# A decoder layer on one core: where a turn of the attention loop spreads and transposes the cross reciprocals, and when it turns the cross keys

## The chip, the cores and the metric

The kernel runs on one core of a Trainium2 chip. The metric is the device time of one execution in microseconds; the time before is the median of three runs. The engines are TensorE (PE, with its weight loads shown apart as PEld), VectorE (DVE), ScalarE (ACT), GpSimd (POOL) and SyncE (SP), which issues the DMAs. Each has its own instruction stream and they meet through semaphores.

## What is computed

A decoder layer with pre-normalisation on 32 sequences of 128 tokens and 512 features, in float32: causal self-attention (16 heads of 32), cross-attention to a context of 128 tokens with 256 features (32 heads of 16), and a gated feed-forward part with quantised weights.

```python
x = x + self_attention(layernorm(x), Wq, Wk, Wv, Wo)       # rope on q and k, causal
x = x + cross_attention(layernorm(x), ctx, pos, Wq, Wkv, Wout, bout)
#   q = (x @ Wq).reshape(b, n, 32, 16);  k, v = split(ctx @ Wkv)
#   q, k = axial_rope(q, pos), axial_rope(k, pos)
#   w = softmax(q . k / sqrt(16));  out = (w @ v) @ Wout + bout
x = x + ffn(layernorm(x))
```

## The kernel before

`build_decoder` has two phases. `attention_phase` takes one sequence at a time; `ffn_phase` then runs over eight blocks of four sequences. The change touches the first alone.

**Turns.** The attention is a software pipeline. A turn, `turn(sq, cq, nx, nz, oq)`, works on four sequences at once: self-attention of `sq`, cross-attention of `cq` (the sequence before it), the projections of the next one, `nx`, and the end of the cross-attention of `oq`, the one before `cq`. `schedule` writes out four turns, loops over 27 (`fori(2, B - 3)`), writes out one more and closes with `last()`. Each engine has a `turn` of its own with its instructions in a fixed order, so the order in the source is the order on the queue. In the loop the values waited for are in registers.

**Scores and probabilities.** A turn computes three sets of scores into the PSUM banks S[0..3]: "1" (self), "2a" and "2b" (the two halves of the cross heads). For each set DVE takes the row maxima (`row_maxima`, L1180), ACT the 16 exponentials with their row sums (`exponentials`, L949), PE transposes the probabilities (`halves_of_probs`, L553), and DVE (banks 0 and 2, L1186) and ACT (banks 1 and 3, L1014) copy them back to SBUF as probT, which the next product and, in the same banks, the next scores wait for (`collect`).

**Transposes in halves.** A 128x128 transpose can be done as 64-row halves. `halves_of_two` does so for two tiles at once, alternating the upper rows of the one with the lower rows of the other into their two banks; the remaining halves may follow only when the first have been written, for which PE waits on its own semaphore `halves_d`. `transpose_keys_and_probs` puts a group of probabilities between the first halves of the two keys and their second ones.

**Reciprocals.** The row sums of both cross halves are inverted by DVE (`row_sums2`, L1200), spread over the 16 columns of each head by POOL (`spread`, L405, tile rbc2), transposed by PE into the bank TC, copied by ACT to rT2 (`copy_reciprocals`, L955), and multiplied into the attention's output by DVE (`context2`). The same chain with rbc1 and rT1 serves self-attention.

**The end of a turn on PE.** `project_v1` (L666) does the value projection in 12 matmuls, 10 of them (`V1_SPLIT`) ahead of `transpose_keys_and_probs` (L578 for the keys, L553 for the probabilities) and 2 behind. Then come the four full transposes of z2, the normalised input of cross-attention (L497), into TC, and the next turn starts with the masks (L521) and matmuls (L526) of the scores "1". Behind these and the product `attend2("2b")` (L648) stand the four transposes of rbc2 (L497), the q2 projection of z2, and the o2 projection (both L512).

**The end of a turn on the others.** DVE: statistics of x1 (the last is L1103), the maxima of "2b", the ropes of k2 and k1 (L1130 and L1133), the normalisation (L1109 to L1114), a copy of the transposed k2 (L1382), the even copies of "2b", the reciprocal. POOL: the sums of both ropes (L399), the masked copies of k2 for even and odd heads (`key_pairs`, L421), the spread of the reciprocals.

Of the kernel before, what the change touches and what calls it, by code (L numbers as in the profile page):

```python
# [138 lines left out]
def attention_phase(nc, fp32, fp32r, ALU, ACT, AX, x, ctx_in, pos, consts,  # L139
                    wq1, wk1, wv1, wo1, wq2, wkv2, wo2, bout, x2_dram, shared_f, shared, ident, mhalf_c, ffn):  # L140
    es = ExitStack()
    with es:
# [229 lines left out]
        def _(pool):  # L372
# [24 lines left out]
            def rope_sum(n, q):  # L397
                wait(pool, ab[n], q + 1)
                pool.tensor_tensor(RA[n][:, :], RA[n][:, :], RB[n][:, :], ALU.add).then_inc(rot[n], 1)  # L399
# [51 lines left out]
            def turn(sq, cq, nx, nz, oq):  # L451
                if is_first(nx):
                    rope_sum("q1", nx)
                    rope_sum("k1", nx)
                if is_first(sq):
                    split_ctx(sq)
                    rope_sum("q1", nx)
                    spread(1, sq, rinv1, rbc1, H1, DK1)
                    rope_sum("k2", sq)
                if oq is not None:  # L460
                    ctx_low(2, oq)
                if cq is not None:
                    rope_sum("q2", cq)
                if nz is not None:
                    rough_rstd(1, nz)
                if sq is not None and cq is not None:
                    spread(1, sq, rinv1, rbc1, H1, DK1)
                    split_ctx(sq)
                if cq is not None:
                    add_bias(cq)  # L470

                if sq is not None:
                    ctx_low(1, sq)
                if nx is not None and cq is not None:
                    rope_sum("q1", nx)
                if sq is not None:
                    rough_rstd(2, sq)
                    if cq is not None:
                        rope_sum("k2", sq)

                if nx is not None and sq is not None:
                    rope_sum("k1", nx)
                if sq is not None:
                    key_pairs(sq)
                if cq is not None:
                    spread(2, cq, rinv2, rbc2, H2, DK2)

# [6 lines left out]
        def _(pe):  # L494
            def transpose4(dst, src, k=KT):
                for j in range(k):
                    last = nc.tensor.transpose(dst[:, j * P:(j + 1) * P], src(j), ident[:, :])  # L497
                return last
# [161 lines left out]
            V1_STEPS = [(a, w, j) for a, w in ((z1T_h, WHI["v1"]), (z1T_h, WLO["v1"]), (z1T_l, WHI["v1"])) for j in range(KT)]  # L660
            V1_SPLIT = 10

# [38 lines left out]
            def turn(sq, cq, nx, nz, oq):  # L701
# [21 lines left out]
                if has_o:  # L723
                    attend2("2b")
                    pe.wait_ge(rb_r[2], oq + 1)
                    if has_c:
                        pe.wait_ge(zT_hi[2], cq + 1)
                        pe.wait_ge(zT_lo[2], cq + 1)
                    transpose4(TC, columns(rbc2[:, :, :].rearrange("p h d -> p (h d)"))).then_inc(ri_d[2], 1)
                if has_c:  # L730
# [11 lines left out]
                if has_c and not is_first(cq):  # L742
                    if has_o:
                        pe.wait_ge(riT_r[2], oq + 1)
                    project(TC, cxT_h, cxT_l, "kv2", CKT, slice(D, 2 * D)).then_inc(pj["v2"], 1)
# [52 lines left out]
                if has_s:  # L798
                    pe.wait_ge(z_r[2], sq + 1)
                    pe.wait_ge(k2T_c, sq + 1)  # L800
                    transpose4(TC, columns(z2)).then_inc(zT_d[2], 1)
                if in_loop:
# [24 lines left out]
            def last():  # L827
# [6 lines left out]
                pe.wait_ge(zT_lo[2], M + 1)  # L834
                transpose_reciprocals(2, N)
                project_q2(M)
                project_o2(N)
                transpose_q2(M)
                transpose_prob("1", L)
                pe.wait_ge(riT_r[2], N + 1)  # L840
                project(TC, cxT_h, cxT_l, "kv2", CKT, slice(D, 2 * D)).then_inc(pj["v2"], 1)
# [70 lines left out]

            LOOP_HALVES = 8
            before = {"n": 0}
# [13 lines left out]
        def _(act):  # L928
# [11 lines left out]

            def exponentials(u, q, banks=range(G)):
                rs = (rsum1, rsum2)[kind(u) - 1]
                if u != "2b" and 0 in banks:
                    wait(act, ri_r[kind(u)], q)
                for c in banks:
                    act.wait_ge(nmax_r[kind(u)], G * nth(u, q) + c + 1)
                    for i in range(G):
                        h = head(u, c, i)
                        last = nc.scalar.activation(prob[:, c, i, :], S[c][:, i * P:(i + 1) * P], ACT.Exp,  # L949
                                                    bias=nmax[:, c, i:i + 1], accum_out=rs[:, h:h + 1])  # L950
                    last.then_inc(p_r[kind(u)], 1)

            def copy_reciprocals(n, q):
                act.wait_ge(ri_d[n], q + 1)
                nc.scalar.activation((rT1, rT2)[n - 1][:, :], TC[:, :], ACT.Copy).then_inc(riT_r[n], 1)  # L955

# [10 lines left out]
            def last():  # L967
                exponentials("1", L, (0,))
                copy_reciprocals(2, N)
                exponentials("1", L, (1, 2, 3))  # L970
                copy_q2(M)
# [48 lines left out]
            def turn(sq, cq, nx, nz, oq):  # L1020
                has_s, has_c, has_n, has_o = sq is not None, cq is not None, nx is not None, oq is not None
                if has_s:
                    exponentials("1", sq, (0,))
                if has_o:
                    copy_reciprocals(2, oq)
                if has_s:
                    exponentials("1", sq, (1, 2, 3))
                if has_c:
# [4 lines left out]
                if has_c:  # L1033
                    copy_v2(cq, TC)
                    exponentials("2a", cq, (0,))
                if has_s:
                    copy_reciprocals(1, sq)
# [4 lines left out]
                if has_c:  # L1042
                    exponentials("2a", cq, (1, 2, 3))
                    odd_copies("2a", cq)
# [18 lines left out]
                if has_s:  # L1063
                    act.wait_ge(zT_d[2], sq + 1)
                    nc.scalar.activation(flat(z2T_h), TC[:, :], ACT.Copy).then_inc(zT_hi[2], 1)
                if is_first(nx):
                    z1T_high(nz)
# [17 lines left out]
        def _(dve):  # L1085
# [223 lines left out]
            def turn(sq, cq, nx, nz, oq):  # L1309
# [58 lines left out]
                if has_s:  # L1368
                    dve.wait_ge(x1_r, sq + 1)
                    statistics(2, x1A, sq)  # L1370

                if has_c:
                    row_maxima("2b", cq, range(G))
                if has_s and has_c:
                    rope("k2", sq, TC, DK2, *axial(sq), 1.0)
                if has_n and has_s and has_c:
                    rope("k1", nx, PA, DK1, cos1, sin1, 1.0)
                if has_s:
                    normalise(2, x1A, z2, sq)
                if has_s:  # L1380
                    dve.wait_ge(rT_d["k2"], sq + 1)
                    nc.vector.tensor_copy(RA["k2"][:, :], TC[:, :]).then_inc(k2T_c, 1)  # L1382
                if has_c:
                    even_copies("2b", cq)
                if has_c:
                    row_sums2(cq)
                if has_s:
# [408 lines left out]
```

## Time and profile before

| what | us |
|---|---|
| median of 3 runs (1676.98 to 1678.65) | 1677.18 |
| the profiled execution's own time | 1680.36 |
| its span, first to last instruction | 1678.5 |
| PE busy | 1625.0 (97%) |
| DVE busy | 1162.9 (69%) |
| ACT busy | 967.3 (58%) |
| POOL busy | 548.4 (33%) |

The time of the profiled execution is its span and 1.9 us around it; it lies 3.2 us above the median. The busy time of PE is modelled from the size of its matmuls, which are pipelined, so a busy PE need not be at its peak. In a row of the timeline the first number is the start in us from the span's start, the second the time from the start of the first to the end of the last instruction of the row, and in brackets stands idle time ahead of it with what ended it.

### The profile page before, as it was taken

To read this page: it belongs to the slowest core of one execution; us is meant where nothing else is said; L and a number is where in the kernel's file an instruction comes from. 1 tells how busy PE (TensorE), PEld (TensorE's weight loads), DVE (VectorE), ACT (ScalarE), POOL (GpSimd) and SP (SyncE) were. 2 spreads that over 40 slices of the span, in tenths; PEclk is the share of its full clock that TensorE was granted. 3 is DMA by queue.
4 is the path that set the end of the run, shared out by engine and by line. 5 is a ranking of instruction groups with operands and counts; after the bars stand their busy time and mean duration, and the time that the engine had idled before them with its cause. 6 is when DMAs were issued, how large, how long until landed. Compare 5 with 4: busy or idle time off the path is not lost. (4 is left out here: it accounts for less than half of the span.)

```text
span 1678.5 us, 42062 instructions
## 1 busy us (share of the span) xinstructions
PE 1625.0 (97%) x15216; PEld 1267.4 (76%) x15216; DVE 1162.9 (69%) x2087; ACT 967.3 (58%) x3847; POOL 548.4 (33%) x535
## 2 busy tenths in 40 slices
PE   6899999999999999999999999998999999999997
PEld 4677777777777777777777777766888888888885
DVE  7788788888888888888888878786744344344332
ACT  5577677777777777777767777675422222222221
POOL 4344443444444444444444444341011011011011
PEclk9999999999999999999999999998999999999999
DMA  6011111111110011111111011022420120120110
GB/s 215 29 32 31 36 34 50 30 30 36 41 43 30 30 36 47 37 30 36 30 54 30 30 36 33 23 70 90 150 76 26 50 75 25 50 75 25 50 50 26
DMA packets 55098, 81.00 MB, mean 48 GB/s; under 512 B 4880, under 2 KB 25488, under 8 KB 55056
## 3 DMA queue, kind: packets, MB, share of 16 engines
q1 hardware_dynamic: 55056, 80.43, 14.7%
q8 instruction: 28, 0.46, 0.1%
q14 instruction: 14, 0.11, 0.0%
HBM read 63.63 MB, written 16.78 MB: 48 GB/s over the span
## 5 line engine op out<-in xcount | busy, mean ns | idle before, releaser
L949 ACT ACTIVATE prob<-bank,nmax 128x128 f32<-128x128 f32 x1536 | 539.9, 408 | 155.8 <-DVE nmax L1180 151.7
L949 ACT ACTIVATION_READ_ACCUMULATOR prob<-bank,nmax 128x1 f32 x1536 | 380.7, 248 | 0.0
L1588 PE MATMUL fbank<-shared,piece_hi 128*128 128x512 f32 x1152 | 280.3, 394 | 0.0
L1180 DVE TENSOR_REDUCE nmax<-bank 128x4 f32<-128x512 f32 x376 | 233.5, 683 | 64.8 <-PE bank L536 51.2
L1588 PEld LDWEIGHTS fbank<-shared,piece_hi 128*128 128x128 f32 x1152 | 215.8, 187 | 53.2
L399 POOL TENSOR_TENSOR rope_buf<-rope_buf 128x512 f32<-128x512 f32 x128 | 165.6, 1303 | 159.7 <-DVE rope_buf L1133 159.6
L1740 DVE SCALAR_TENSOR_TENSOR h<-fbank,su_c,sil 128x512 f32<-128x512 f32 x88 | 66.0, 750 | 200.1 <-PE fbank L1588 197.1
L1674 ACT ACTIVATE sil<-fbank,sg_c 128x512 f32<-128x512 f32 x88 | 60.5, 687 | 174.8 <-PE fbank L1588 172.2
L1680 ACT ACTIVATE h_h<-h 128x512 fp32r<-128x512 f32 x88 | 55.6, 632 | 175.1 <-DVE h L1740 175.1
L449 POOL TENSOR_TENSOR cn_l<-cn,cn_h 128x512 fp32r<-128x512 f32 x64 | 82.8, 1294 | 211.9 <-DVE cn L1172 211.9
L512 PE MATMUL bank<-shared,z1T_h 128*128 128x512 f32 x520 | 140.4, 412 | 4.5 <-ACT shared L932 2.6
L1186 DVE COPY probT<-bank 128x512 f32<-128x512 f32 x186 | 119.3, 683 | 23.4 <-PE bank L553 23.3
L1571 POOL TENSOR_TENSOR xr<-xr,ys 128x512 f32<-128x512 f32 x32 | 40.2, 1288 | 288.9 <-DVE ys L1760 288.9
L553 PE MATMUL bank<-ident,prob 64*128 64x64 f32 x2976 | 133.8, 226 | 0.4 <-ACT prob L949 0.4
L553 PEld LDWEIGHTS bank<-ident,prob 64*128 64x128 f32 x2976 | 117.6, 138 | 13.3 <-issue 12.3
L1014 ACT ACTIVATE probT<-bank 128x512 f32<-128x512 f32 x186 | 101.4, 601 | 41.7 <-PE bank L553 41.7
L512 PEld LDWEIGHTS bank<-shared,z1T_h 128*128 128x128 f32 x520 | 93.8, 190 | 34.8 <-issue 12.9
L1603 PE MATMUL fbank<-piece_hi,h_h 128*128 128x512 f32 x288 | 115.3, 400 | 0.5 <-DVE h_l L1743 0.5
L1603 PE MATMUL fbank<-piece_hi,h_l 128*128 128x512 f32 x288 | 113.6, 395 | 0.0
L1743 DVE TENSOR_TENSOR h_l<-h,h_h 128x512 fp32r<-128x512 f32 x88 | 62.9, 715 | 61.4 <-ACT h_h L1680 61.4
L421 POOL TENSOR_TENSOR kT<-rope_buf,cst 128x512 f32<-128x512 f32 x62 | 63.2, 1040 | 62.7 <-DVE rope_buf L1382 62.7
L536 PE MATMUL bank<-kT,qT 32*128 32x256 f32 x1024 | 77.2, 403 | 5.5 <-DVE probT L1186 1.9
(178 smaller groups left out, 3170.2 us busy)
## 6 DMA issues: line engine op xcount, KB each, us to landing
xA<-in_x SPq DMA_DIRECT2D x32, 256.0 KB, 3.1
xB<-in_x SPq DMA_DIRECT2D x32, 256.0 KB, 3.0
x_scratch<-x SPq DMA_DIRECT2D x32, 256.0 KB, 2.0
shared_loaded<-x_scratch SPq DMA_DIRECT2D x8, 1024.0 KB, 7.7
xr<-x_scratch SPq DMA_DIRECT2D x8, 1024.0 KB, 5.7
out<-xr SPq DMA_DIRECT2D x8, 1024.0 KB, 4.3
cx<-in_ctx SPq DMA_DIRECT2D x32, 128.0 KB, 2.2
range_window<-in_wg SPq DMA_DIRECT2D x27, 112.0 KB, 2.0
```

The source lines that it names most:

```text
L399: pool.tensor_tensor(RA[n][:, :], RA[n][:, :], RB[n][:, :], ALU.add).then_inc(rot[n], 1)
L449: pool.tensor_tensor(cn_l[:, :, :], cn[:, :, :], cn_h[:, :, :], ALU.subtract).then_inc(cn_lo[n], 1)
L512: last = nc.tensor.matmul(dst[:, :], a[:, j, :], w[:, j, cols], start=(n == 0), stop=(n == 3 * k - 1))
L536: last = nc.tensor.matmul(S[g][:, 2 * P * i:2 * P * (i + 1)], qT2[rows, j, :], kT2[rows, j, :, :].rearrange("p e t -> p (e t)"), start=Tru ...
L553: last = nc.tensor.transpose(S[c][:, i * P + rows.start:i * P + rows.stop], prob[rows, c, i, :], ident[rows, rows])
L949: last = nc.scalar.activation(prob[:, c, i, :], S[c][:, i * P:(i + 1) * P], ACT.Exp, bias=nmax[:, c, i:i + 1], accum_out=rs[:, h:h + 1])
L1014: nc.scalar.activation(probT[:, c, :, :].rearrange("p g t -> p (g t)"), S[c][:, :], ACT.Copy).then_inc(pTo_r[kind(u)], 1)
L1180: nc.vector.tensor_reduce(out=nmax[:, c, :], in_=S[c][:, :].rearrange("p (g k) -> p g k", g=G), op=ALU.max, axis=AX, negate=True).then_inc ...
L1186: nc.vector.tensor_copy(probT[:, c, :, :].rearrange("p g t -> p (g t)"), S[c][:, :]).then_inc(pTe_r[kind(u)], 1)
L1588: last = nc.tensor.matmul(dst[:, :], w[:, k, cols], z[:, k, :], start=(n == 0), stop=(n == len(passes) * KT - 1))
L1603: last = nc.tensor.matmul(DN[s][:, :], a[j % 2][:, tok], w[piece][:, j % 2, :], start=(j == 0 and n == 0), stop=(j == HT - 1 and n == len( ...
L1740: nc.vector.scalar_tensor_tensor(out=h[j % 2][:, :], in0=UP[j % 2][:, :], scalar=su_c[:, j:j + 1], in1=sil[j % 2][:, :], op0=ALU.mult, op1 ...
```

## The change

Six edits in the attention phase:

1. PE no longer transposes rbc2 behind the scores of the next turn. At the turn's end it transposes z2 (into TC) and rbc2 (into PA, PSUM bank 4) together in halves, first halves and then second halves, with nothing between. `last()` loses one group of transposes too. The wait for ACT's copy of the reciprocals (`riT_r[2]`) moves ahead of the q2 projection, which writes PA.
2. `V1_SPLIT` is 9 in place of 10: one value matmul more stands behind the transposes of keys and probabilities.
3. POOL spreads the reciprocals ahead of the masked key copies.
4. ACT copies the transposed reciprocals rT2 at the turn's end, between the copies of z2 and v1, in place of within the exponentials "1" of the next turn. The copy of rT1 within the exponentials "2a" comes ahead of the first bank's fourth exponential in place of behind it.
5. DVE does the rope of k2 ahead of the row maxima of "2b".
6. DVE takes the reciprocal of the cross row sums ahead of the copy of k2 and the even copies.

```diff
                 if nx is not None and sq is not None:
                     rope_sum("k1", nx)
+                if cq is not None:
+                    spread(2, cq, rinv2, rbc2, H2, DK2)
                 if sq is not None:
                     key_pairs(sq)
-                if cq is not None:
-                    spread(2, cq, rinv2, rbc2, H2, DK2)
...
-            V1_SPLIT = 10
+            V1_SPLIT = 9
...
                     attend2("2b")
-                    pe.wait_ge(rb_r[2], oq + 1)
-                    if has_c:
-                        pe.wait_ge(zT_hi[2], cq + 1)
-                        pe.wait_ge(zT_lo[2], cq + 1)
-                    transpose4(TC, columns(rbc2[:, :, :].rearrange("p h d -> p (h d)"))).then_inc(ri_d[2], 1)
+                    pe.wait_ge(riT_r[2], oq + 1)
...
+                if has_s and has_c:
+                    pe.wait_ge(rT_r["k1"], nx + 1)
+                    pe.wait_ge(rb_r[2], cq + 1)
+                    tiles = ((TC, z2), (PA, rbc2[:, :, :].rearrange("p h d -> p (h d)")))
+                    z, r = second_halves_of_two(tiles, first_halves_of_two(tiles))
+                    z.then_inc(zT_d[2], 1)
+                    r.then_inc(ri_d[2], 1)
+                elif has_s:
                     transpose4(TC, columns(z2)).then_inc(zT_d[2], 1)
...
-            LOOP_HALVES = 8
+            LOOP_HALVES = 9
...
                     for i in range(G):
+                        if c == 0 and i == G - 1 and between is not None:
+                            copy_reciprocals(*between)
...
                 if has_s:
-                    exponentials("1", sq, (0,))
-                if has_o:
-                    copy_reciprocals(2, oq)
-                if has_s:
-                    exponentials("1", sq, (1, 2, 3))
+                    exponentials("1", sq)
...
                     copy_v2(cq, TC)
-                    exponentials("2a", cq, (0,))
-                if has_s:
+                    exponentials("2a", cq, between=(1, sq))
+                elif has_s:
                     copy_reciprocals(1, sq)
...
                     nc.scalar.activation(flat(z2T_h), TC[:, :], ACT.Copy).then_inc(zT_hi[2], 1)
+                if has_c:
+                    copy_reciprocals(2, cq, PA)
...
-                if has_c:
-                    row_maxima("2b", cq, range(G))
                 if has_s and has_c:
                     rope("k2", sq, TC, DK2, *axial(sq), 1.0)
+                if has_c:
+                    row_maxima("2b", cq, range(G))
...
                     normalise(2, x1A, z2, sq)
+                if has_c:
+                    row_sums2(cq)
...
                     even_copies("2b", cq)
-                if has_c:
-                    row_sums2(cq)
```

On PE, the end of a loop turn before, behind the transposes of the probabilities (bank 7 is TC, bank 4 is PA; z2 and rbc2 are the normalised input and the spread reciprocals):

```order
L666 MATMUL bank6<-shared,z1T_l 128x512 x2
L497 MATMUL bank7<-ident,z2 128x128 [waits k2T_copied,z2_ready]
L497 MATMUL bank7<-ident,z2 128x128 x3
L919 REGISTER_ALU
L919 COMPARE_AND_BRANCH
```

and now:

```order
L666 MATMUL bank6<-shared,z1T_l 128x512 x3
L578 MATMUL bank7<-ident,z2 128x64 [waits rinv2_spread,k1T_ready,z2_ready,k2T_copied]
L578 MATMUL bank4<-ident,rbc2 128x64
L578 MATMUL bank7<-ident,z2 128x64
L578 MATMUL bank4<-ident,rbc2 128x64
L578 MATMUL bank7<-ident,z2 128x64
L578 MATMUL bank4<-ident,rbc2 128x64
...
L588 REGISTER_ALU
L578 MATMUL bank4<-ident,rbc2 128x64 [waits first_halves_transposed]
L578 MATMUL bank7<-ident,z2 128x64
L578 MATMUL bank4<-ident,rbc2 128x64
...
L920 REGISTER_ALU
L920 COMPARE_AND_BRANCH
```

The four full transposes of z2 have become two groups of eight halves with those of rbc2, of which the second group's first half waits for the first group.

On DVE, the stretch of the loop turn from the last statistics of x1 to the k1 rope, before:

```order
L1103 TENSOR_SCALAR ve2<-mv2 128x1 [waits mean_var2_ready]
L1179 REGISTER_ALU
L1180 TENSOR_REDUCE nmax<-bank0 128x4 [waits scores2_done]
L1180 TENSOR_REDUCE nmax<-bank1 128x4 [waits scores2_done]
L1180 TENSOR_REDUCE nmax<-bank2 128x4 [waits scores2_done]
L1180 TENSOR_REDUCE nmax<-bank3 128x4 [waits scores2_done]
L1130 ISA [waits rope_q1_ready,k2_transposed,proj_k2_done]
L1130 SCALAR_TENSOR_TENSOR rope_buf<-bank7,cos2 128x512
L1133 REGISTER_ALU
L1133 SCALAR_TENSOR_TENSOR rope_buf<-bank7,sin2 128x512
L1130 SCALAR_TENSOR_TENSOR rope_buf<-bank4,cst 128x512 [waits rope_q2_ready,k1_transposed,proj_k1_done]
L1133 SCALAR_TENSOR_TENSOR rope_buf<-bank4,cst 128x512
```

and now:

```order
L1101 TENSOR_SCALAR ve2<-mv2 128x1 [waits mean_var2_ready]
L1128 ISA [waits rope_q1_ready,k2_transposed,proj_k2_done]
L1128 SCALAR_TENSOR_TENSOR rope_buf<-bank7,cos2 128x512
L1131 REGISTER_ALU
L1131 SCALAR_TENSOR_TENSOR rope_buf<-bank7,sin2 128x512
L1177 REGISTER_ALU
L1178 TENSOR_REDUCE nmax<-bank0 128x4 [waits scores2_done]
L1178 TENSOR_REDUCE nmax<-bank1 128x4 [waits scores2_done]
L1178 TENSOR_REDUCE nmax<-bank2 128x4 [waits scores2_done]
L1178 TENSOR_REDUCE nmax<-bank3 128x4 [waits scores2_done]
L1128 SCALAR_TENSOR_TENSOR rope_buf<-bank4,cst 128x512 [waits rope_q2_ready,k1_transposed,proj_k1_done]
L1131 SCALAR_TENSOR_TENSOR rope_buf<-bank4,cst 128x512
```

The rope of k2 (L1130 and L1133 before, now L1128 and L1131) stands ahead of the four row maxima (L1180, now L1178).

On POOL, at each turn's end (rope sums L399, spread L405, masked keys L421):

```order
 L399 TENSOR_TENSOR rope_buf<-rope_buf 128x512 x2
+L405 TENSOR_TENSOR rbc2<-rinv2,one_c 128x512
 L421 TENSOR_TENSOR kT2<-rope_buf,cst 128x4x128 x2
-L405 TENSOR_TENSOR rbc2<-rinv2,one_c 128x512
```

The spread has moved ahead of the two masked copies.

## Rows read from the trace of the kernel before

**Rows 1.** Who PE waited for, whole span: total us, times, longest.
```profile
PE bank L521 <- DVE probT L1186: 5.5, 27, 0.2
```

**Rows 2.** Timeline of PE about one turn's end: start, length, what.
```profile
606.10 2.13 PE L666 MATMUL bank<-shared,z1T_h 128*128 128x512 f32 x8
608.07 0.63 PE L666 MATMUL bank<-shared,z1T_l 128*128 128x512 f32 x2
608.63 0.46 PE L578 MATMUL bank<-ident,rope_buf 64*128 64x64 f32 x8
...
609.53 1.08 PE L553 MATMUL bank<-ident,prob 64*128 64x64 f32 x24
610.53 0.73 PE L666 MATMUL bank<-shared,z1T_l 128*128 128x512 f32 x2
611.10 0.60 PE L497 MATMUL bank<-ident,z 128*128 128x128 f32 x4
611.89 0.44 PE L521 MATMUL bank<-causal,ident_b 32*32 32x512 bf16 x16 [0.19 <-DVE probT L1186]
...
614.37 0.66 PE L497 MATMUL bank<-ident,rbc 128*128 128x128 f32 x4
614.78 1.18 PE L512 MATMUL bank<-w_q_hi,z2T_h 128*128 128x512 f32 x4
...
646.62 0.44 PE L521 MATMUL bank<-causal,ident_b 32*32 32x512 bf16 x16 [0.21 <-DVE probT L1186]
```

**Rows 3.** Timeline of PE, end of the first turn, with no group between.
```profile
53.72 0.69 PE L578 MATMUL bank<-ident,rope_buf 64*128 64x64 f32 x8
54.56 0.47 PE L578 MATMUL bank<-ident,rope_buf 64*128 64x64 f32 x8 [0.15 <-PE bank L578]
54.96 0.72 PE L666 MATMUL bank<-shared,z1T_l 128*128 128x512 f32 x2
```

**Rows 4.** Timelines of DVE and PE at the first boundary behind the loop.
```profile
1096.63 1.28 DVE L1186 COPY probT<-bank 128x512 f32<-128x512 f32 x2
...
1097.97 0.44 PE L521 MATMUL bank<-causal,ident_b 32*32 32x512 bf16 x16
```

**Rows 5.** Timeline of DVE about the same turn's end as rows 2.
```profile
601.62 0.15 DVE L1103 TENSOR_SCALAR ve<-mv 128x1 f32<-128x1 f32 x1
602.23 2.48 DVE L1180 TENSOR_REDUCE nmax<-bank 128x4 f32<-128x512 f32 x4 [0.46 <-PE bank L536]
604.63 0.68 DVE L1130 SCALAR_TENSOR_TENSOR rope_buf<-bank,cos 128x512 f32<-128x512 f32 x1
...
606.43 0.68 DVE L1133 SCALAR_TENSOR_TENSOR rope_buf<-bank,cst 128x512 f32<-128x512 f32 x1
...
610.37 1.28 DVE L1186 COPY probT<-bank 128x512 f32<-128x512 f32 x2
611.56 0.34 DVE L1200 RECIPROCAL rinv<-rsum 128x32 f32<-128x32 f32 x1
```

**Rows 6.** Timelines of PE and DVE at the q2 rope, in and before the loop.
```profile
616.74 1.10 PE L512 MATMUL bank<-w_q_hi,z2T_l 128*128 128x512 f32 x4
617.99 0.69 DVE L1130 SCALAR_TENSOR_TENSOR rope_buf<-bank,cos 128x512 f32<-128x512 f32 x1 [0.34 <-PE bank L512]
...
95.64 1.10 PE L512 MATMUL bank<-w_q_hi,z2T_l 128*128 128x512 f32 x4
96.78 0.69 DVE L1130 SCALAR_TENSOR_TENSOR rope_buf<-bank,cos 128x512 f32<-128x512 f32 x1 [0.28 <-PE bank L512]
```

**Rows 7.** Timeline of ACT, first and last of the exponentials "2b".
```profile
602.96 0.37 ACT L949 ACTIVATE prob<-bank,nmax 128x128 f32<-128x128 f32 x1 [2.29 <-DVE nmax L1180]
...
608.35 0.29 ACT L949 ACTIVATION_READ_ACCUMULATOR prob<-bank,nmax 128x1 f32 x1
```

**Rows 8.** Timeline of POOL about the same turn's end.
```profile
605.99 2.53 POOL L399 TENSOR_TENSOR rope_buf<-rope_buf 128x512 f32<-128x512 f32 x2 [3.59 <-DVE rope_buf L1133]
...
612.52 1.04 POOL L405 TENSOR_TENSOR rbc<-rinv,one_c 128x512 f32<-128x512 f32 x1
```

More of the change, by code:

```diff
@@ L742, in turn @@
                 if has_c and not is_first(cq):
-                    if has_o:
-                        pe.wait_ge(riT_r[2], oq + 1)
                     project(TC, cxT_h, cxT_l, "kv2", CKT, slice(D, 2 * D)).then_inc(pj["v2"], 1)
@@ L834, in last @@
                 pe.wait_ge(zT_lo[2], M + 1)
-                transpose_reciprocals(2, N)
+                pe.wait_ge(riT_r[2], N + 1)
                 project_q2(M)
@@ L839, in last @@
                 transpose_prob("1", L)
-                pe.wait_ge(riT_r[2], N + 1)
                 project(TC, cxT_h, cxT_l, "kv2", CKT, slice(D, 2 * D)).then_inc(pj["v2"], 1)
@@ L939, in z1T_high, with exponentials @@
                 nc.scalar.activation(flat(z1T_h), PC[:, :], ACT.Copy).then_inc(zT_hi[1], 1)
-            def exponentials(u, q, banks=range(G)):
+            def exponentials(u, q, banks=range(G), between=None):
                 rs = (rsum1, rsum2)[kind(u) - 1]
@@ L951, in exponentials, with copy_reciprocals @@
                     last.then_inc(p_r[kind(u)], 1)
-            def copy_reciprocals(n, q):
+            def copy_reciprocals(n, q, src=TC):
                 act.wait_ge(ri_d[n], q + 1)
-                nc.scalar.activation((rT1, rT2)[n - 1][:, :], TC[:, :], ACT.Copy).then_inc(riT_r[n], 1)
+                nc.scalar.activation((rT1, rT2)[n - 1][:, :], src[:, :], ACT.Copy).then_inc(riT_r[n], 1)
             def copy_v2(q, src):
@@ L967, in last @@
             def last():
-                exponentials("1", L, (0,))
-                copy_reciprocals(2, N)
-                exponentials("1", L, (1, 2, 3))
+                exponentials("1", L)
                 copy_q2(M)
@@ L1022, in turn @@
                 if has_s:
-                    exponentials("1", sq, (0,))
-                if has_o:
-                    copy_reciprocals(2, oq)
-                if has_s:
-                    exponentials("1", sq, (1, 2, 3))
+                    exponentials("1", sq)
                 if has_c:
@@ L1042, in turn @@
                 if has_c:
-                    exponentials("2a", cq, (1, 2, 3))
                     odd_copies("2a", cq)
@@ L1370, in turn @@
                     statistics(2, x1A, sq)
+                if has_s and has_c:
+                    rope("k2", sq, TC, DK2, *axial(sq), 1.0)
                 if has_c:
                     row_maxima("2b", cq, range(G))
-                if has_s and has_c:
-                    rope("k2", sq, TC, DK2, *axial(sq), 1.0)
                 if has_n and has_s and has_c:
```

## The prediction

> **What bounds the kernel now.** I read the views in this order: who waited for whom on PE, then the order of time on PE at the end of one loop turn, then VectorE (DVE), ScalarE (ACT) and GpSimd (POOL) in the same stretch, then two places outside the loop in which the new code's situations already occur. The waits [rows 1] say that PE in the 27 loop turns waits for one thing only, 0.2 us a turn, at the first matmuls of the next turn's scores (L521), and that it is DVE's copy of the transposed probabilities that ends it. Nothing else of weight is waited for in the loop, so PE's own order of work sets the turn, 34.73 us from one L521 group to the next (611.89 and 646.62, [rows 2]), and the change is worth what it takes off or puts on PE's line. Everything else counts only where it makes PE wait.
>
> [Rows 2] is that line: value projection (8 matmuls from 606.10, two more from 608.07), the half transposes of the two keys with the probabilities between them (608.63 to 610.53), the last two value matmuls, the four full transposes of z2 (611.10), and the next turn's scores at 611.89. Then, 2.5 us later, the four full transposes of the reciprocals rbc2 (614.37), with the q2 projection at 614.78.
>
> **The change part by part.** All times are those of the turn boundary at 611.89; the price per turn is then taken 30 times (the 27 loop turns, the two turns before the loop that have both inputs, and the turn after it; all four-transpose groups that go are 30 as well, the last of them in the closing block).
>
> *Removed: the rbc2 transposes behind the scores.* 614.78 - 614.37 = 0.41 us of PE [rows 2], nothing beside them. The wait for ACT's copy of the reciprocals now stands ahead of the q2 projection; that copy is now made before the first exponentials, in ACT time that was idle, and 2.5 us lie between. Value -0.41. The product on DVE that needed this copy moves up too, by about as much as the projection that reads it.
>
> *Replaced: four z2 transposes by 16 half transposes of z2 and rbc2.* Before, z2 took 611.89 - 611.10 = 0.79 us up to the scores. That is not four transposes' worth: the same four cost 0.41 in the rbc2 rows, the rest is the wait for DVE, whose copies end at 610.37 + 1.28 = 611.65, 0.24 before PE starts. So there is slack of up to 0.38 in which more work would be free, and this is what speaks for the change. But groups of eight half transposes cost 0.30 each: three of them lie between 608.63 and 609.53. They cost so little only because another group stands between a pair's first and second halves. In the new code nothing does, and the second halves wait for the first to have come back. The first turn has this case: first halves at 53.72, the second at 54.56, next matmul at 54.96 [rows 3]. The first group lasted 0.69 there against 0.46 at 608.63, so 0.23 of the 0.84 is a slow start that the loop does not have: first to second 0.61, and 0.40 from there to the next kind of work, 1.01 in all. As its lower end I take 0.94 (if the gap of 0.15 between the two groups were half as long in the loop), and add what the loop's turn end costs. That is read from DVE's last copy to PE's scores: 0.24 in the loop, and after the loop, with waits on constants, 1096.63 + 1.28 = 1097.91 to 1097.97, 0.06 [rows 4]. The difference, 0.18, is the sequencer's work on register values and the branch. Before it hid partly under the wait; now all of it can stand behind the second halves. So 0.94 to 1.19, I take 1.10, against 0.79: +0.31 (0.15 to 0.40).
>
> The Trainium skill, "TensorE: Matmul & The Clock Gate", section "Measured speedup vs the span model", gives for matmuls in different row groups some 4 ns from one start to the next; eight halves would then be issued in 0.03 us, an estimate from that page, and the sum would be 0.4 to 0.5 us a turn better. The groups of this kernel, 0.30 each [rows 2], show that it doesn't hold for alternating halves, and the rows decide. "Perfetto Trace Analysis", section "Tensor Engine Instruction (MATMUL, LD_WEIGHTS)", says that PE's reported end lies ahead of the acknowledgement and of the semaphore; the 0.15 us between the first group's end (53.72 + 0.69 = 54.41) and the second's start agrees [rows 3].
>
> *Moved on DVE: k2's rope ahead of the third row maxima.* DVE ends its statistics at 601.62 + 0.15 = 601.77 and then waits 0.46 for the scores [rows 5]. The rope's two halves (0.60 from start to start: three steps from 604.63 to 606.43) now go into this hole. They don't start at once: in the loop the rope reads its tables at a register's address, and starts 0.15 after PE's modelled end (616.74 + 1.10 = 617.84, rope at 617.99), where outside it starts 0.04 after (95.64 + 1.10 = 96.74, rope at 96.78) [rows 6]. So rope at 601.88, maxima at 603.08 instead of 602.23: 0.85 later. The k1 rope is done 0.4 earlier.
>
> *What is queued behind it.* ACT's 16 exponentials follow the maxima at once and back to back: 602.96 to 608.35 + 0.29 = 608.64 [rows 7]. They now end at 609.49. PE needs the last two banks of them for the group at 609.53. Before there were 0.89 us of slack; now, because V1_SPLIT is 9, PE is there one value matmul earlier (608.07 - 606.10 over 8 = 0.25), at 609.28. ACT's end plus 0.1 for the semaphore gives 609.59: PE waits 0.30 in a place where it did not. Bounds: 0 (if the rope really fills only the hole and PE arrives no earlier) to 0.35. The value matmul itself moves, and costs nothing.
>
> *POOL.* Its rope sums took 605.99 to 608.52 [rows 8], and PE's key transposes came at 608.63, 0.11 behind. Now k1's sum begins when DVE's k1 rope ends (601.88 + 1.20 + 2.40 + 1.20 = 606.68, and 0.08 until the write ends), so at about 606.8, and lasts half of 2.53: 608.1. PE wants it at 608.38. No wait, and this is what the earlier rope buys: without it, V1_SPLIT 9 would wait here. The reciprocal (0.34, [rows 5]) waits for ACT at 609.49, so the spread (1.04, [rows 8]) runs 609.9 to 611.0. PE wants it at 611.40. The cover is about 0.2 once the loop's register wait is counted. The key masks, now behind the spread, are wanted only at the second scores of the next turn.
>
> *DVE's copies.* k2's copy, one copy of 0.6 us ahead of the probability copies at 610.37 [rows 5], had started at about 609.76, held by PE; it now stands behind the reciprocal, which starts at 609.53, so at 609.8, the same. The probability copies cannot start before the second halves of the first pair are done: PE at 609.59 + 0.60, and 0.2 until DVE sees it, 610.4. They end near 611.7, so DVE would release the scores at about 611.97. The other chain on PE: 609.59 + 1.00 to the value matmuls, three of them 0.81 (two took 0.57, one more 0.24), z2 at 611.40, and 1.10 more: 612.50. PE's own line ends last; the wait on DVE goes.
>
> *ACT.* The reciprocals' copy within the first exponentials of "2a" comes one exponential earlier; PE's q1 projection follows directly and sets the next step, so nothing.
>
> *Sum per turn:* z2 starts 0.30 later; +0.31 from there to the scores; -0.41 behind them: +0.20 (ends: 0 + 0.15 - 0.41 = -0.26 and 0.35 + 0.40 - 0.41 = +0.34). Times 30: +6.0 us (-7.8 to +10.2). The profiled execution took 1680.36 us (span 1678.5), 3.2 above the median of 1677.18; against its own time 1686.4, and as a median 1683.2.
>
> **The rivals.**
>
> *The slack takes it up: faster.* The turn's end has 0.38 us that are no work, and if the branch and the register waits run under the half transposes (then 0.94 for the pair), and ACT is at most 0.1 late, the sum is 0.10 + 0.15 - 0.41 = -0.16 a turn, -4.8 us: 1672.4. For it: PE had idle time of 0.2 at the boundary and PE work falls from two groups of 0.41 to two of 0.30. Against it: the first turn's row for the pair without a group between. It decides below 0.41 for delay and pair together. Chance 0.22.
>
> *It cancels: same.* The pair costs 0.31 more but ACT's lateness is only 0.1, since PE too reaches the keys later than I count (its 0.11 behind POOL shows how near that is): 0.00 a turn, 1677. Chance 0.28.
>
> *The spread comes late: slower by more.* Reciprocal and spread hang behind the last exponential. If they are done 0.2 after PE wants them, each turn loses 0.2 more, +0.40, +12 us: 1689. For it: a cover of 0.2; against it: it was worked out with every step at its measured length. Chance 0.08.
>
> *The change doesn't do what it says* would be k1's rope sum ending no earlier, so that PE waits for POOL at 608.4 and nothing is won by V1_SPLIT 9; then z2 starts at most as late as in my sum, and the result is the forecast's, 1683.
>
> **How the numbers follow.** Forecast (+0.20 a turn, 1683) has chance 0.42. A measurement can tell about 0.2%, 3.4 us, from no change. Slower: the forecast and the late spread, 0.50. Same: 0.28. Faster: 0.22. The range takes the faster rival's time and most of the forecast's upper end, 1672.5 to 1688.0, and leaves out the late spread and a gain beyond 0.16 a turn.
>
> **What would show it.** In the changed profile the turn should last 34.9 us against 34.73. Right: PE waits for ACT's probabilities ahead of the second group of "2b" (some 0.2 idle, ACT's last exponential ending about 609.5 in a turn whose scores began at 611.89 before), and a gap of about 0.15 between the two groups of z2 and rbc2, with PE waiting for itself; DVE's copy no longer ends the wait at L521. Wrong: first maxima less than 0.6 us later than before, no wait for ACT, second halves less than 0.5 after the first, or scores less than 0.9 after the first z2 half. Then the turn is shorter than 34.73 and the faster rival holds.

## The result, and the profile after

The changed kernel takes 1696.24 us (median, 1695.49 to 1697.13) against 1677.14 for the kernel before: a ratio of 1.0108, 95% interval 1.0096 to 1.0120. It is slower, as forecast, but by 19 us where 6 were forecast, and outside the range. The profiled execution took 1695.89 us, with a span of 1694.1.

The waits of PE in the changed kernel, as in [rows 1] (total us, times, longest):

```profile
PE bank L521 <- issue: 11.3, 26, 0.5
...
PE bank L578 <- POOL rope_buf L399: 7.6, 29, 1.4
PE bank L578 <- PE bank L578: 4.6, 30, 0.2
PE bank L553 <- ACT prob L952: 4.1, 23, 0.5
```

DVE's copy no longer ends a wait at L521. In its place stands an idle time of the same instruction that nothing releases ("issue"), 26 times, and 27 loop turns jump back 26 times. The last two lines are the two waits that the prediction named: PE for itself in all 30 pairs, PE for ACT's last exponentials, which the profile names 23 times. The line with POOL is new by name (before: 1.4, 1, 1.4) and costs nothing: it is q2's rope sum ahead of the transposes of q2, and from the q2 projection to these PE takes 6.11 us (623.83 to 629.94), before 6.10 (614.78 to 620.88).

The end of one turn on PE, the counterpart of [rows 2] (start, length, what). The gap at L521 stands in that place behind all 26 jumps back, 0.43 to 0.46 us long:

```profile
614.39 2.13 PE L666 MATMUL bank<-shared,z1T_h 128*128 128x512 f32 x8
616.36 0.40 PE L666 MATMUL bank<-shared,z1T_l 128*128 128x512 f32 x1
616.69 0.46 PE L578 MATMUL bank<-ident,rope_buf 64*128 64x64 f32 x8
...
617.31 0.47 PE L578 MATMUL bank<-ident,rope_buf 64*128 64x64 f32 x8
617.92 1.08 PE L553 MATMUL bank<-ident,prob 64*128 64x64 f32 x24 [0.15 <-ACT prob L952]
618.93 0.97 PE L666 MATMUL bank<-shared,z1T_l 128*128 128x512 f32 x3
619.83 0.27 PE L578 MATMUL bank<-ident,z 64*128 64x64 f32 x1
...
620.45 0.24 PE L578 MATMUL bank<-ident,rbc 64*128 64x64 f32 x1 [0.15 <-PE bank L578]
...
620.69 0.22 PE L578 MATMUL bank<-ident,z 64*128 64x64 f32 x1
621.35 0.44 PE L521 MATMUL bank<-causal,ident_b 32*32 32x512 bf16 x16 [0.43 <-issue]
...
623.83 1.19 PE L512 MATMUL bank<-w_q_hi,z2T_h 128*128 128x512 f32 x4
```

The scores before these began at 585.84, so the turn lasts 35.51 us, 0.78 more than the 34.73 of [rows 2]. The mean of the 26 intervals between the 27 loop turns is 35.50 against 34.75, and 26 times 0.75 is 19.4 us, the loss. Step by step, this turn against that of [rows 2]:

| stretch on PE | before | after | difference |
|---|---|---|---|
| keys' first halves to the group of 24 probabilities | 0.90 | 1.23 | +0.33 |
| that group to the last value matmuls | 1.00 | 1.01 | +0.01 |
| value matmuls ahead of and behind the keys, 2 and 2, now 1 and 3 | 0.56 + 0.57 | 0.33 + 0.90 | +0.10 |
| z2 (now with rbc2) to the scores | 0.79 | 0.62 + 0.90 | +0.73 |
| scores to the q2 projection | 2.89 | 2.48 | -0.41 |

They make +0.76. The first row is alike in every turn of the loop: 1.22 to 1.25 us, before 0.89 or 0.90. The same second group in a place without a jump, the boundary of two turns written out one after the other, with the start of the scores behind it:

```profile
89.13 0.24 PE L578 MATMUL bank<-ident,rbc 64*128 64x64 f32 x1 [0.16 <-PE bank L578]
...
89.53 0.43 PE L521 MATMUL bank<-causal,ident_b 32*32 32x512 bf16 x16
```

0.40 us from the one to the other, exactly what [rows 3] gave; behind a jump back it is 0.90. This half microsecond is what the forecast lacked.

DVE and ACT did what was worked out. On DVE, to compare with [rows 5]:

```profile
609.92 0.15 DVE L1101 TENSOR_SCALAR ve<-mv 128x1 f32<-128x1 f32 x1
610.14 0.69 DVE L1128 SCALAR_TENSOR_TENSOR rope_buf<-bank,cos 128x512 f32<-128x512 f32 x1
...
611.35 2.48 DVE L1178 TENSOR_REDUCE nmax<-bank 128x4 f32<-128x512 f32 x4
...
618.08 0.63 DVE L1382 COPY rope_buf<-bank 128x512 f32<-128x512 f32 x1
618.67 1.29 DVE L1184 COPY probT<-bank 128x512 f32<-128x512 f32 x2
```

From the last statistics to the maxima it is 1.43 us, before 0.61: 0.82 later (0.85 worked out). The copies end at 619.96, 1.4 us ahead of the scores, so DVE has nothing to do with the gap.

### The profile page after: what moved, and what is told of

It is laid out like the page before. It is cut to its first block and busy times, and to the rows that moved or that the text cites. A ratio compares the mean times of both kernels' runs of the same rounds, so it can differ in the third digit from the quotient of the medians.

```text
span 1694.1 us, 42603 instructions
## 1 busy us (share of the span) xinstructions
PE 1621.1 (96%) x15456; PEld 1260.7 (74%) x15456; DVE 1156.0 (68%) x2087; ACT 972.9 (57%) x3847; POOL 549.5 (32%) x535
## 5 line engine op out<-in xcount | busy, mean ns | idle before, releaser
L952 ACT ACTIVATION_READ_ACCUMULATOR prob<-bank,nmax 128x1 f32 x1536 | 374.3, 244 | 0.0
L1178 DVE TENSOR_REDUCE nmax<-bank 128x4 f32<-128x512 f32 x376 | 233.3, 684 | 56.1 <-PE bank L536 37.2
L399 POOL TENSOR_TENSOR rope_buf<-rope_buf 128x512 f32<-128x512 f32 x128 | 167.0, 1305 | 157.7 <-DVE rope_buf L1131 157.6
L405 POOL TENSOR_TENSOR rbc<-rinv,one_c 128x512 f32<-128x512 f32 x64 | 66.5, 1039 | 87.9 <-DVE rinv L1198 67.8
```

Source lines behind the costliest of these rows:

```text
L405: pool.tensor_tensor(tile[:, :, :], r[:, :].unsqueeze(2).to_broadcast([P, h, w]), one_c[:, :].unsqueeze(2).to_broadcast([P, h, w]), ALU.mu ...
L1178: nc.vector.tensor_reduce(out=nmax[:, c, :], in_=S[c][:, :].rearrange("p (g k) -> p g k", g=G), op=ALU.max, axis=AX, negate=True).then_inc ...
```

## The experiments

The theory after the result, A, which is an inference that the runs have to bear out: PE's sequencer reads ahead of the array. In the kernel before it passes the loop's jump while the four transposes of z2 are still at work. In the changed kernel the last thing ahead of the jump hangs on PE's own semaphore, so the jump begins only when that has been met, and there is too little work left to hide it.

**The wait alone, in the kernel before (e4).**

```diff
                     transpose4(TC, columns(z2)).then_inc(zT_d[2], 1)
+                    pe.wait_ge(zT_d[2], sq + 1)
```

> The kernel before with one wait more: behind the four full transposes of z2, as the last thing of a turn, PE waits on its own semaphore (that they are done). No half transposes, nothing moved. Theory A (in the changed kernel the loop's jump back stands behind a wait of PE on itself, so PE cannot run ahead over it, and its cost of about 0.5 us, seen as the idle time put down to issue, shows at each of the 26 jumps): z2's transposes end at 611.70, 0.15 for the wait, 0.6 to the scores instead of 611.89: +0.5 us a turn, 1677 + 13 to 15 = about 1691. Rival B (the gap belongs to the two interleaved groups of halves or to the order of the other engines): at most 0.1 us a turn, below 1680.

Measured: 1698.43 us, 1.0127 of before (1.0110 to 1.0144), as much as the whole change (the intervals overlap; the mean turn is 35.41 us, in the changed kernel 35.50). The waits of PE:

```profile
PE bank L521 <- PE bank L497: 23.5, 28, 0.9
```

and one turn's end in its timeline:

```profile
618.93 0.60 PE L497 MATMUL bank<-ident,z 128*128 128x128 f32 x4
620.38 0.44 PE L521 MATMUL bank<-causal,ident_b 32*32 32x512 bf16 x16 [0.85 <-PE bank L497]
```

1.45 us from z2 to the scores instead of 0.79. At a boundary that is written out, the same wait leaves 0.75 (z2 at 88.81, scores at 89.56). No half transpose and no rope has been moved here, so the gap doesn't belong to them, and e4's rival B falls. It was more than worked out, since 0.70 and not 0.6 pass from the release (619.53 + 0.15) to the scores.

**A wait in the same place that is long met (e10), and an own wait one step earlier (e9).** What of that is the instruction, what the standing still, what the place? First e10's edit, then e9's:

```diff
                     transpose4(TC, columns(z2)).then_inc(zT_d[2], 1)
+                    pe.wait_ge(z_r[2], sq + 1)
```
```diff
+                    pe.wait_ge(pj["v1"], nx + 1)
                     transpose4(TC, columns(z2)).then_inc(zT_d[2], 1)
```

> The kernel before with a wait in the place of e4's, as the last thing of a turn, but on DVE's z2, which has been there for two microseconds, so that nothing is stood still for. Theory A: PE's sequencer passes it early and runs ahead over the jump as before, 1677 to 1679. Rival D (any wait at the jump, with the register arithmetic for its value, costs the gap, whether it holds PE up or not): above 1685.

> The kernel before with PE's wait on itself one step earlier than in e4: ahead of the four transposes of z2, for the end of the value projection, instead of behind them. Theory A (an own wait costs its 0.15 us and the drain, and what makes it dear in e4 is the jump behind it): the transposes, 0.41, now run beside the jump. z2 starts at 611.4 instead of 611.1, the scores 0.7 behind the release as in e4 (there 1.45 from the start of z2 less 0.75), at 612.1 instead of 611.89: +0.2 to +0.25 us a turn, 1683 to 1685. Rival C (a wait of PE on itself costs 0.7 us in the loop wherever it stands, by the register's value it compares with): as e4, 1698.

Measured: e10 1677.82 us, 0.9996 (0.9986 to 1.0006), with the gap before L521 as in the kernel before; e9 1688.26 us, 1.0061 (1.0042 to 1.0081). So a wait at the jump, with the register arithmetic for its value, is free as long as it holds nothing up. The own wait of e9 costs 0.31 where it stands (z2 starts 0.88 behind the two value matmuls, before 0.57), and in e9 less is left of the idle time ahead of the scores (PE's timeline):

```profile
615.88 0.73 PE L666 MATMUL bank<-shared,z1T_l 128*128 128x512 f32 x2
616.76 0.63 PE L497 MATMUL bank<-ident,z 128*128 128x128 f32 x4
617.59 0.44 PE L521 MATMUL bank<-causal,ident_b 32*32 32x512 bf16 x16 [0.20 <-issue]
```

The turn is 35.09 us, and the loss half of e4's. That is above the 1683 to 1685 expected: from the release to the scores it is 0.83, not 0.70. Rival C, by which e9 would be as slow as e4, falls.

**Which edit loses (e2, e3, e1).** e2 is the changed kernel with the rope's place and V1_SPLIT as before; e3 the kernel before with these two edits alone; e1 the changed kernel with only the rope's place undone:

```diff
-                if has_s and has_c:
-                    rope("k2", sq, TC, DK2, *axial(sq), 1.0)
                 if has_c:
                     row_maxima("2b", cq, range(G))
+                if has_s and has_c:
+                    rope("k2", sq, TC, DK2, *axial(sq), 1.0)
```

> The changed kernel with the rope of k2 behind the row maxima again and V1_SPLIT 10 again: the half transposes of z2 and rbc2 at the turn's end, with what POOL, ACT and DVE's reciprocal need for it, are left. If gap at the jump and wait for ACT are separate causes that add up: the wait for ACT goes (0.33 us in 23 turns), the 0.73 us that the pair takes more than z2 stays, less 0.41: +0.3 us a turn against before, about 1686, and the gap of 0.43 at L521 unchanged. If the pair is the whole loss: about 1695, as the changed kernel. If the rope's place is the whole loss: 1667 to 1677.

> The kernel before with the rope of k2 ahead of the third row maxima and V1_SPLIT 9, nothing else. Expected where the causes add up: PE waits 0.3 us for ACT's last exponentials ahead of the second group of probabilities, z2 starts 0.3 to 0.4 us later, and the turn is 0.3 longer: 1684 to 1687, together with e2 about the loss of the changed kernel. Rival (the slack of the turn's end, where PE waits for DVE, takes most of it up): at most 0.1 a turn, up to 1680.

> The changed kernel with the rope of k2 behind the row maxima again, V1_SPLIT still 9. ACT is no longer late. But the sum of k1's rope on POOL ends as late as before (608.52 against PE at 608.38), so PE should wait some 0.15 to 0.25 for POOL ahead of the keys, and three value matmuls instead of two lie behind: 0.25 to 0.35 us a turn slower than e2, about 1694, no better than the changed kernel. If POOL's end does not bind, as e2, 1686.

Measured: e2 1687.23 us, 1.0058 (1.0041 to 1.0075); e3 1679.50 us, 1.0012 (1.0003 to 1.0022); e1 1696.07 us, 1.0116 (1.0099 to 1.0133). e2 and e1 came within 2.1 us of what was expected (1686 and 1694): the pair alone costs 0.38 us a turn (a mean of 35.13 against 34.75), with the idle time of 0.44 at L521 unchanged, and with V1_SPLIT 9 but the rope late, PE comes to the keys 0.56 behind the ninth value matmul instead of 0.33. The profile puts the idle time there down to issue; k1's rope sum on POOL ends at 614.68, 0.10 ahead of the keys at 614.78, before it was 0.11 [rows 8].

e3 did not. PE does come to the 24 probabilities late by much the same, 0.32 (642.79 to 643.39, 0.60 where 0.28 lay between). But the rest of the turn's end on PE in e3 is:

```profile
642.79 0.46 PE L578 MATMUL bank<-ident,rope_buf 64*128 64x64 f32 x8
643.39 1.08 PE L553 MATMUL bank<-ident,prob 64*128 64x64 f32 x24
644.40 0.96 PE L666 MATMUL bank<-shared,z1T_l 128*128 128x512 f32 x3
645.20 0.60 PE L497 MATMUL bank<-ident,z 128*128 128x128 f32 x4
645.72 0.43 PE L521 MATMUL bank<-causal,ident_b 32*32 32x512 bf16 x16
```

From z2 to the scores it is 0.52 instead of 0.79: the delay comes out of the time in which PE waited for DVE's copies, and the mean turn is 34.81 us, 0.06 longer. So the two losses of 9 and 1.5 us don't add up to 19. Alone, the late exponentials are absorbed; with the pair, the slack that absorbs them is gone and they cost their 0.33 in full (35.50 against e2's 35.13 a turn).

**The same place with full transposes (e5, e6).** Four of z2 and four of rbc2, no own wait. e6 has the rope's place and V1_SPLIT as before besides:

```diff
-                    z, r = second_halves_of_two(tiles, first_halves_of_two(tiles))
-                    z.then_inc(zT_d[2], 1)
-                    r.then_inc(ri_d[2], 1)
+                    transpose4(TC, columns(z2)).then_inc(zT_d[2], 1)
+                    transpose4(PA, columns(rbc2[:, :, :].rearrange("p h d -> p (h d)"))).then_inc(ri_d[2], 1)
```

> The changed kernel with the 16 half transposes of z2 and rbc2 at the turn's end replaced by four full ones of z2 and four of rbc2, in the same place; all else (ropes, V1_SPLIT 9, the order on POOL, ACT and DVE) as changed. More work for PE by its own length (0.82 against 0.60 us), but no wait of PE on itself. Theory A (what costs is the jump behind PE's own wait): PE runs ahead over the jump, the idle time put down to issue at L521 goes, from the first z2 transpose to the scores it takes 0.93 us (0.41 for rbc2 and the 0.52 that z2 takes in e3 where nothing waits) instead of 1.52, the turn is 0.6 shorter than in the changed kernel: 1679 to 1681. Rival B (the jump costs its 0.5 us wherever PE's work at the turn's end has no slack): 0.82 and 0.65 follow each other, 1.5 as in the changed kernel, about 1696.

> As e5, and the rope of k2 behind the maxima and V1_SPLIT 10 as before. Then ACT is not late either. z2 starts as early as in the kernel before, 0.93 to the scores in place of 0.79, and 0.41 less behind them: -0.27 us in 30 turns, 1677 - 8 = 1669, faster than both kernels. If the copies of DVE (they end 0.55 behind the start of z2) or the spread of POOL bind: between 1669 and 1677.

Measured: e5 1681.19 us, 1.0013 (1.0002 to 1.0024), as expected and 15 us less than the changed kernel with more work on PE; e6 1671.86 us, 0.9961 (0.9946 to 0.9976), faster than both kernels. PE in e6:

```profile
607.59 0.60 PE L497 MATMUL bank<-ident,z 128*128 128x128 f32 x4
608.02 0.60 PE L497 MATMUL bank<-ident,rbc 128*128 128x128 f32 x4
608.55 0.43 PE L521 MATMUL bank<-causal,ident_b 32*32 32x512 bf16 x16
```

It takes 0.96 from z2 to the scores, with no idle time ahead of them; the turn is 34.46 us. In e5 it is 0.96 to 0.97 behind every jump and the turn 34.82, so here too, where nothing is left to absorb it, the rope's place with V1_SPLIT 9 costs some 0.35 a turn. Rival B (another than e4's: the jump shows wherever the turn's end has no slack) falls.

**Value matmuls between and behind the halves (e7, e8).** e7 is the changed kernel with its three last value matmuls set one ahead of the first halves, one between the groups, one behind; e8 has the rope's place and V1_SPLIT as before, with one between and one behind. e8's edit on PE, with its conditions left out (the two value matmuls ahead of the first halves go):

```diff
-                    z, r = second_halves_of_two(tiles, first_halves_of_two(tiles))
+                    ready = first_halves_of_two(tiles)
+                    project_v1(range(V1_SPLIT, V1_SPLIT + 1))
+                    z, r = second_halves_of_two(tiles, ready)
...
+                    project_v1(range(V1_SPLIT + 1, len(V1_STEPS))).then_inc(pj["v1"], 1)
```

> The changed kernel with its three last value matmuls spread: one ahead of the first halves of z2 and rbc2, one between first and second halves, one behind, ahead of the jump. Theory A: no wait of PE on itself (0.15 less), and the last matmul (0.24) covers part of the jump, so that 0.2 of the 0.43 idle at L521 is left; the first halves may wait for POOL's spread, which comes 0.4 us earlier than PE reached them: 0.25 to 0.4 us a turn less than changed, 1685 to 1689. Rival B: only the 0.15 goes, 1692.

> The ropes in the old order and V1_SPLIT 10, first halves of z2 and rbc2 directly behind the probabilities, then one value matmul, second halves, the last value matmul, the jump. Against the kernel before: from the end of the probabilities' transposes to the scores 0.30 + 0.33 + 0.40 + 0.34 = 1.37 us and 0 to 0.2 of the jump left over, against 1.36 before (0.57 for two value matmuls and 0.79), and 0.41 less behind the scores: -0.2 to -0.4 a turn, 1665 to 1671 (theory A). Rival B: 0.5 stays in full, +0.1 a turn, 1680.

Measured: e7 1697.29 us, 1.0111 (1.0095 to 1.0128); e8 1683.07 us, 1.0028 (1.0018 to 1.0037). Both missed. PE in e8:

```profile
611.78 1.05 PE L553 MATMUL bank<-ident,prob 64*128 64x64 f32 x24
613.10 0.24 PE L578 MATMUL bank<-ident,z 64*128 64x64 f32 x1 [0.26 <-POOL rbc L405]
...
613.49 0.50 PE L666 MATMUL bank<-shared,z1T_l 128*128 128x512 f32 x1
613.92 0.27 PE L578 MATMUL bank<-ident,rbc 64*128 64x64 f32 x1
...
614.31 0.50 PE L666 MATMUL bank<-shared,z1T_l 128*128 128x512 f32 x1
614.75 0.43 PE L521 MATMUL bank<-causal,ident_b 32*32 32x512 bf16 x16
```

The idle time of PE for itself is gone and so is that at L521, in both kernels. But a group of eight halves takes 0.39 with a value matmul behind it, not 0.30, and a single value matmul 0.43, not the 0.25 that it takes in a row of its kind: every change of kind costs some 0.1 to 0.2, and that used up what was won. In e8 PE waits for the spread as well, and in e7 it idles 0.18 ahead of the first halves, which the profile puts down to issue (28 times). Both times lie nearer to rival B's than to theory A's, but by rival B the 0.5 of the jump would stand in full, and it doesn't: 613.92 to 614.75 is 0.83, and at e8's last boundary, where nothing jumps, the same instructions take 0.82 (1102.88 to 1103.70).

**The same boundary with and without a jump.** The kernels' own written-out turns separate the jump further. The table has the time on PE up to the first matmul of the scores (L521), in us. The loop's last turn ends in the same instructions and the same wait as the others, but runs on instead of jumping back. Only at the jump back and into the loop are the values that the next turn waits for in registers; behind the last turn they are constants.

| kernel, from | written out, ahead of the loop | into the loop | 26 jumps back | out of the loop | written out, behind it |
|---|---|---|---|---|---|
| changed, second halves | 0.40 | 0.60 | 0.89 to 0.93 | 0.49 | 0.39 |
| e4, z2 | 0.75 | 1.19 | 1.44 to 1.53 | 1.08 | 0.67 |
| e9, z2 | 0.56 | 0.73 | 0.83 to 0.91 | 0.56 | 0.56 |
| e6, z2 | 0.97 | 0.96 | 0.96 to 0.97 | 0.96 | 0.97 |
| e8, first halves | 1.65 | 1.65 | 1.64 to 1.66 | 1.64 | 1.64 |

Where the own wait stands last, a jump back takes 0.41 (changed kernel) and 0.37 (e4) more than running out of the loop; where enough work stands between (e6, e8) all five places are alike, so the loop costs nothing there. But the half microsecond isn't all jump: running into the loop, with no jump, already costs 0.20 in the changed kernel and 0.44 in e4 over the written-out boundary ahead of it. The loop's set-up and the register arithmetic at its head are candidates for that, and no run takes the arithmetic and the jump apart.

## Why the prediction was wrong

The forecast had the sign and most of its terms, and its sum failed in one step, the way from the second halves over the loop's jump to the scores. A smaller term was left out.

- *Removed transposes, -0.41.* Right: 2.89 to 2.48.
- *k2's rope ahead of the maxima, and ACT late.* Right: maxima 0.82 later, PE 0.33 later at the group of 24 (0.30 forecast), in all the loop's turns. ACT ends at 617.78 and PE starts at 617.92, 0.14 for the 0.1 that was put down for the semaphore. The lower bound was 0.
- *V1_SPLIT.* "The value matmul itself moves, and costs nothing" was right: in e3 the stretches ahead of and behind the keys and probabilities are 0.32 and 0.80, together 1.12, before 1.13 (0.56 and 0.57). The term that was put at nothing without a reason is the step from the value matmuls to the halves: three of them take 0.90 ahead of the pair against 0.80 ahead of full transposes (e3), two take 0.66 (e2) against 0.57. That is +0.1 a turn for the pair, a change of kind as in e8.
- *First to second halves, 0.61.* Right: 0.62.
- *From the second halves to the scores: 0.40 and up to 0.18 for the loop, of which about 0.09 was taken in the value.* This step failed. It measured 0.90. The 0.18 had been read from how much later PE starts behind DVE's last copy in the loop than outside. But there PE stands at the head of the next turn when the copy ends, and the row shows only what lies after that wait; that the jump had been passed by then is an inference, which e3, e6 and e10 bear out, since in them a jump with transposes ahead of it adds nothing. A jump that other work hides left no mark in these traces (e6: 0.96 with it, 0.97 without), so its price could not be read from such a row. The boundary of [rows 4] is besides the second behind the loop, not the first: at the first the copies end at 1063.38 and the scores start at 1063.52, 0.14 later and not 0.06. So the upper end of the whole pair (1.19) was not an upper end. It measured 1.52.
- *The slack of 0.38.* What stood at the turn's end was 0.27 of it (0.79 against 0.52 in e3). It was counted once, as something that the pair uses up, which was right. That the late exponentials would by themselves have been nearly free (e3, +1.5 us) was not seen, but the sum did not need it, since it set both in one turn.
- *The half transposes by themselves.* Of the short step from one matmul's start to the next the prediction says that "it doesn't hold for alternating halves". That is true of a group, not of a pair: in the changed kernel both halves of a pair start at 619.83, and the next pairs follow at 619.94, 620.00 and 620.07.
- *POOL and DVE.* Right: no wait for the spread (its write ends at 619.35, PE comes at 619.83) or for the key sums, and DVE's wait gone, as the prediction's last part asked for.
- *The rivals.* The faster one is refuted by the second halves to the scores. The cancelling one needed ACT only 0.1 late. The late spread, the dearest, gave +12 us, nearest to the loss of 19, but was not its cause: PE did not wait for the spread.

With 0.90 in place of 0.49 in that step, and the 0.1 ahead of the pair, the forecast's own sum would have been 0.7 us a turn, close to the mean of 0.75 measured. It would still have been too much by 0.4 in the four pairs behind which nothing jumps back.

## What to carry to other kernels

Do not let the last thing ahead of a loop's jump be a wait of the engine on itself that really holds it up (waits on other engines in that place were not tried, but for one long met); put work behind it, or do the work in a form that needs no wait, even if it is longer by itself (eight full transposes at 0.82 us beat sixteen halves at 0.60 here by 15 us). Slack at the end of a turn can be spent once: test edits alone and together, since what is nearly free alone (e3, +1.5 us) costs its full length when another edit has used the slack. And before an interval is taken as a bound, ask whether the thing it is to bound happened within it.

## What the runs showed of the hardware

A jump of PE costs nothing while PE has enough queued work (e6: 0.96 to 0.97 from z2 to the scores with a jump and without, e8: 1.64 to 1.66, and e10 with 0.9996 of the time before). When PE has been held up by its own wait just ahead of it, the same instructions take 0.90 instead of 0.40, of which 0.41 is what jumping back takes more than running out of the loop (0.49). From the release of PE's own wait to the first matmul behind the jump it took 0.70 us (e4, nothing between), 0.83 (e9, four full transposes) and 0.90 (changed kernel, eight halves); at the written-out boundaries ahead of the loop, counted in the same way, 0.00, 0.56 and 0.40. That it grows so little with the work between fits a jump that runs beside that work.

At the entry of the loop, where PE runs into it from above, the changed kernel needs 0.60 (second halves at 123.70, scores at 124.30), so running into the loop is cheaper than jumping back. What the time goes into is open in part: the branch and the register arithmetic behind it are not taken apart by any run. A fetch of instructions over the DMA queues it is not: between 165 and 1047 us, where PE jumps back at least 24 times, the trace of the changed kernel has no packet of an instruction queue at all.
